# Attention scores as fp32 products of 32 rows in four banks, one projection per unit, and the weights W_ih loaded and split early

## The reference, cut to what matters

```python
xn = rms_norm(x, g_norm) * (1 + scale) + shift         # x [16, 256, 512], scale and shift from cond @ W_emb
q, k, v = split(xn @ W_qkv)                             # 16 heads, d = 32
logits = rms_norm(q, g_q) @ rms_norm(k, g_k).T * d ** -0.5
o = softmax(logits) @ v
x1 = x + o + o @ W_out
gi = x1 @ W_ih + b_ih                                   # GRU, 256 steps one after the other
r, z = sigmoid(gi_r + h_r), sigmoid(gi_z + h_z)         # h_* from h @ W_hh + b_hh
n = tanh(gi_n + r * h_n)
h = (1 - z) * n + z * h
out = x1 + h
```

## Time and profile before

| what | value |
|---|---|
| median of 3 runs | 1945.35 us (1941.71 to 1947.37) |
| the profiled execution, its own time | 1951.58 us |
| its span, first to last instruction | 1949.8 us |
| PE busy | 1796.5 us, 92% |
| DVE busy | 1285.5 us, 66% |
| ACT busy | 855.8 us, 44% |
| POOL busy | 391.2 us, 20% |
| mean granted TensorE clock | 0.969 of full |

### The profile page before, as it was taken

One profiled execution on the slowest core, in us unless ns is written; L12 is line 12 of the kernel. 1 busy time (PEld: TensorE's weight loads), 2 busy tenths in 40 slices (PEclk: granted clock), 3 DMA queues, 4 the chain that ended last, 5 costly groups with the idle time before them and its releaser, 6 DMA issues.

```text
span 1949.8 us, 59362 instructions
## 1 busy us (share of the span) xinstructions
PE 1796.5 (92%) x23337; PEld 1279.7 (66%) x23337; DVE 1285.5 (66%) x5150; ACT 855.8 (44%) x3116; POOL 391.2 (20%) x473
## 2 busy tenths in 40 slices
PE   5699999999999999588999999999999999999996
PEld 4577777777777777455666666666666666666663
DVE  4687777777777777544666666666666666666665
ACT  2466665566665655522333333333333333333333
POOL 3333333333333332110111111111111111111111
PEclk8799999999999999788999999999999999999999
DMA  5555554545544454623434343434343343434341
GB/s 192 129 134 127 124 125 121 127 120 126 122 123 119 121 128 115 174 50 77 76 75 67 74 77 67 81 69 78 67 76 65 76 73 67 83 67 78 62 69 16
DMA packets 155069, 185.94 MB, mean 95 GB/s; under 512 B 18124, under 2 KB 116632, under 8 KB 154792
## 3 DMA queue, kind: packets, MB, share of 16 engines
q1 hardware_dynamic: 154792, 182.14, 43.0%
HBM read 73.01 MB, written 41.94 MB: 59 GB/s over the span
## 4 chain that ended last, share of the span: by engine, by line
PE 86%; issue 4%; DVE 3%; DMA 3%; SPq 2%; POOL 1%; ACT 1%; POOLq 0%; DVEq 0%
PE ps L673 37%; PE ps L654 16%; PE ps L424 13%; PE ps L460 5%; PE ps L496 4%; PE ps L480 3%; PE ps L449 3%; PE ps L486 2%; PE ps L432 1%; SPq L260 1%; DVE xf L702 1%; DMA wst<-in_L_cond_W_ih_dram 1%; DMA GI<-gscr 1%; PE ps L506 1%; PE ps L412 1%
## 5 line engine op out<-in xcount | busy, mean ns | idle before, releaser
L673 PE MATMUL ps<-whh,hT 128*32 128x192 f32 x16384 | 753.4, 329 | 26.4 <-DVE hT L965 13.9
L673 PEld LDWEIGHTS ps<-whh,hT 128*32 128x32 f32 x16384 | 486.7, 110 | 297.7 <-issue 80.2
L1247 POOL TENSOR_TENSOR outG<-hG,GI 128x128 f32<-128x128 f32 x256 | 116.5, 455 | 1038.1 <-DVE hG L958 1038.1
L1138 ACT ACTIVATE v<-ps 128x128 f32<-128x128 f32 x512 | 139.5, 272 | 413.7 <-PE ps L673 413.7
L937 DVE SCALAR_TENSOR_TENSOR v<-v,ps 128x64 f32<-128x64 f32 x512 | 111.0, 217 | 285.0 <-ACT v L1138 285.0
L1142 ACT ACTIVATE v<-v 128x64 f32<-128x64 f32 x512 | 131.2, 256 | 304.5 <-DVE v L945 304.5
L742 DVE TENSOR_REDUCE nmx<-ps 128x2 f32<-128x512 f32 x256 | 175.2, 685 | 116.8 <-PE ps L449 115.7
L1041 ACT ACTIVATE P<-ps,nmx 128x256 f32<-128x256 f32 x512 | 240.9, 483 | 8.6 <-DVE nmx L742 8.6
L1190 POOL TENSOR_TENSOR rq<-msq,mh 128x16 f32<-128x16 f32 x64 | 187.2, 2925 | 5.4 <-POOL msq L1186 0.2
L954 DVE TENSOR_TENSOR v<-v,v 128x64 f32<-128x64 f32 x512 | 115.1, 225 | 105.7 <-ACT v L1142 105.7
L449 PE MATMUL ps<-kst,qst 128*128 128x256 f32 x512 | 130.7, 339 | 47.5 <-issue 47.5
(11 more groups left out here) (107 smaller groups left out, 2506.0 us busy)
## 6 DMA issues: line engine op xcount, KB each, us to landing
gscr<-nat SPq DMA_DIRECT2D x96, 256.0 KB, 2.7
GI<-gscr SPq DMA_DIRECT2D x128, 192.0 KB, 6.6
kst<-kh SPq DMA_DIRECT2D x128, 128.0 KB, 2.4
kst<-kl SPq DMA_DIRECT2D x128, 128.0 KB, 2.4
qst<-qh SPq DMA_DIRECT2D x128, 128.0 KB, 2.5
qst<-ql SPq DMA_DIRECT2D x128, 128.0 KB, 2.4
xb<-in_x_dram SPq DMA_DIRECT2D x16, 512.0 KB, 4.9
xres<-in_x_dram SPq DMA_DIRECT2D x32, 256.0 KB, 3.2
```

The costliest lines, as they stand in the source:

```text
L673: last = pe.matmul(ps[32 * j:32 * j + 32, q, 0:192], hT[:, 32 * c:32 * c + 32], whg[:, c, :, 128 * j + 64 * q:128 * j + 64 * q + 64], star ...
L1138: s.activation(v_rz[:, q, :], ps[:, q, 64:192], ACT.Tanh, scale=0.5).then_inc(s_tr, 1)
```

## The change

- Scores: no parts and no stacks. The turned q and k are kept as fp32, `qT` and `kT`, for two batches. `scores(U)` makes four products of 32 rows, one for each head of the unit, from partitions 32j to 32j+31, each into its own bank (0 to 3), after both exponential pairs of the unit before.
- The banks: `PASS` uses banks 7 and 6; `pO` and `pR` move into bank 5, single, beside the second half of the turned probabilities, so `turn_p` waits for `scale` of the unit before.
- The order: PE makes scores(U+1), `turn_p(U)`, the fillers (at most one projection or output projection in a unit), `times_v(U)`. DVE takes `scale(U-1)` first, then both maxima, its copy, the reciprocals, and only then what belongs to the fillers. The turned q and k are copied by ACT (`keep_turned`) in place of DVE. `raw` and its square are two steps on ACT.
- `xh` and `xl` are double. The squares of x have a tile of their own, `xsq`.
- W_ih is loaded when batch 1 begins and one of its 12 blocks is split in each of the batches 2 to 13.
- After the last unit the input products for the first 16 steps are made (72 matmuls) before the GRU starts; the other 1080 pieces are laid 4 or 5 to a step.

```diff
-        PASS += [("turn", _n, 0, 1), ("project", _n, 0, 0), ("turn", _n, 1, 1), ("project", _n, 1, 0), ("turn", _n, 0, 0),
-                 ("project", _n, 0, 2), ("turn", _n, 1, 0), ("project", _n, 1, 2)]
+        PASS += [("turn", _n, 0, 1), ("project", _n, 0, 0), ("turn", _n, 1, 1), ("project", _n, 1, 0), ("project", _n, 0, 2)]
     if _m < NB:
-        PASS += [("rows", _m, 0), ("rows", _m, 1)]
+        PASS += [("rows", _m, 0)]
+    if _n < NB:
+        PASS += [("turn", _n, 0, 0), ("project", _n, 1, 2)]
+    if _m < NB:
+        PASS += [("rows", _m, 1)]
     PASS += [("out", _b, 0)]
-BANK = {p: (7, 3)[k % 2] for k, p in enumerate(PASS)}
+BANK = {p: (7, 6)[k % 2] for k, p in enumerate(PASS)}
...
+            def scores(U):
                 b, c, i = U // 8, U % 4, U % 8 // 4
...
+                if U:
+                    pe.wait_ge(s_ex, 2 * U)
+                for j in range(4):
+                    q = slice(32 * j, 32 * j + 32)
+                    last = pe.matmul(pS[j], qT[b % 2][q, i, c, :], kT[b % 2][q, :, c, :], start=True, stop=True)
                 last.then_inc(s_S, 1)
...
+            scores(0)
             for U in range(NU):
                 b, u = U // 8, U % 8
                 n, m = b + 1, b + 2
                 if U + 1 < NU:
-                    scores(U + 1, 0)
-
+                    scores(U + 1)
+                turn_p(U)
+                if u == 0 and b:
+                    passed(("turn", b, 1, 0))
+                elif u == 2 and b:
+                    passed(("out", b - 1, 1))
+                elif u == 5 and n == NB or u == 7 and n < NB:
+                    passed(("out", b, 0))
                 if n < NB:
                     if u == 0:
                         passed(("project", n, 0, 1))
-                    elif u == 2:
+                    elif u == 1:
+                        passed(("project", n, 1, 1))
+                    elif u == 3:
                         passed(("turn", n, 0, 1))
                         passed(("project", n, 0, 0))
-                    elif u == 3:
+                    elif u == 4:
+                        passed(("turn", n, 1, 1))
                         passed(("project", n, 1, 0))
-                    elif u == 4:
+                    elif u == 5:
                         passed(("project", n, 0, 2))
-                    elif u == 5:
+                        if m < NB:
+                            passed(("rows", m, 0))
+                    elif u == 6:
+                        passed(("turn", n, 0, 0))
                         passed(("project", n, 1, 2))
...
+                        if m < NB:
+                            passed(("rows", m, 1))
+                times_v(U)
...
+            for tt in range(2):
+                for g in range(3):
+                    for k in range(GP):
+                        gate_piece(tt, g, k)
+                turn_x1(tt + 1, F[2])
...
+                if U:
+                    scale(U - 1)
                 if U + 1 < NU:
                     maxima(U + 1, 0)
                     maxima(U + 1, 1)
...
                 if U:
                     low(U - 1)
...
+                if b and u == 0:
+                    out_sum(b - 1, 0)
+                elif b and u == 3:
+                    out_sum(b - 1, 1)
+                if n < NB:
+                    if u == 1:
+                        squares(n, 0, 1)
+                    elif u == 2:
+                        squares(n, 1, 1)
+                        normalize(n, 0, 1)
+                    elif u == 3:
+                        normalize(n, 1, 1)
+                    elif u == 4:
+                        squares(n, 0, 0)
+                        if m < NB:
+                            x_scale(m)
+                    elif u == 5:
+                        squares(n, 1, 0)
+                        normalize(n, 0, 0)
+                    elif u == 6:
+                        if m < NB:
+                            affine(m, 0, BANK["rows", m, 0])
+                        normalize(n, 1, 0)
+                    elif u == 7:
+                        if m < NB:
+                            affine(m, 1, BANK["rows", m, 1])
+                        if 2 <= b < 2 + 3 * KC:
+                            wih_low((b - 2) // KC, (b - 2) % KC)
```

More of the change, by code:

```diff
@@ L32 @@
     _n, _m = _b + 1, _b + 2
+    if _b:
+        PASS += [("turn", _b, 1, 0)]
     if _n < NB:
@@ L143, in cond_resid_kernel @@
         E = sb("E", [128, NB])
[L144 removed]
+        assert base[0] <= a_qk
         base[0] = a_P
@@ L320, in _ @@
             load_x(1)
-            stack(0, 1)
-            stack(0, 0)
             for b in range(NB):
[L325 to L329, removed]
+                if b + 2 < NB:
+                    load_x(b + 2)
+                if b == 1:
+                    sp.wait_ge(s_wsd, 3)
+                    sp.wait_ge(s_ss, 1)
                     for g in range(3):
@@ L367, in _ @@
                         sp.dma_start(whh[32 * j:32 * j + 32, :, D:3 * D], w[:, :, 0:2 * D]).then_inc(s_lwh, 16)
+                if b:
+                    store_x1(b - 1, 0)
+                    load_residual(b - 1, 1)
+                    store_x1(b - 1, 1)
+                load_residual(b, 0)
+            store_x1(NB - 1, 0)
+            load_residual(NB - 1, 1)
+            load_x1(0)
+            load_x1(1)
+            load_gx(0)
+            load_x1(2)
+            store_x1(NB - 1, 1)
+            for g in range(3):
+                store_gate(0, g)
+            load_g(0)
+            load_x1(3)
+            for g in range(3):
+                store_gate(1, g)
+            load_g(1)
+            load_x1(4)
             o_v = out.rearrange("b (t s) (j f) -> t j b s f", s=ST, j=4)
@@ L555, in passed @@
                     out_proj(*a)
-            def first_gate(g):
-                bank = (7, 3, 7)[g]
-                if g == 0:
-                    emptied(pe, ("out", NB - 1, 0))
-                    pe.wait_ge(s_1c, 2)
-                    pe.wait_ge(s_wsl, 3 * KC)
-                elif g == 2:
-                    pe.wait_ge(s_gb, 1)
-                for c in range(KC):
-                    for m, (xp, wp) in enumerate(((x1h, wih_h), (x1l, wih_h), (x1h, wih_l))):
-                        last = pe.matmul(ps[:, bank, :], xp[:, 0, c, :], wp[:, c, g * D:(g + 1) * D],
-                                         start=(c == 0 and m == 0), stop=(c == KC - 1 and m == 2))
-                last.then_inc(s_g, 1)
-            scores(0, 0)
-            scores(0, 1)
+            scores(0)
             for U in range(NU):
@@ L617, in _ @@
-                turn_p(U)
-                if u == 5 and m < NB:
-                    passed(("rows", m, 0))
-                if n == NB:
-                    if u == 4:
-                        passed(("out", b, 0))
-                    elif u == 5:
-                        emptied(pe, ("out", b - 1, 1))
-                        turn_x1(0, ps[:, 3, :])
-                    elif u == 6:
-                        first_gate(1)
-            times_v(NU - 1)
+                        if m < NB:
+                            passed(("rows", m, 1))
@@ L657, in gate_piece @@
                     last.then_inc(s_g, 1)
+            emptied(pe, ("out", NB - 1, 0))
+            emptied(pe, ("out", NB - 2, 1))
+            turn_x1(0, F[2])
+            passed(("out", NB - 1, 1))
+            for tt in range(2):
+                for g in range(3):
+                    for k in range(GP):
+                        gate_piece(tt, g, k)
+                turn_x1(tt + 1, F[2])
             first_seed()
@@ L928, in _ @@
             low(NU - 1)
+            x1_low(0, F[2])
+            out_sum(NB - 1, 1)
+            for tt in range(2):
+                for g in range(3):
+                    keep_gate(tt, g, F[(3 * tt + g) % 2])
+                x1_low(tt + 1, F[2])
             for t in range(T):
@@ L1022, in keep_raw, with keep_turned @@
                 s.activation(sq[:, i, :], raw[:, i, :], ACT.Square).then_inc(s_sq, 1)
+            def keep_turned(b, i, g):
+                bank = BANK["turn", b, i, g]
+                r = ps[:, bank, :].rearrange("p (c t) -> p c t", c=KC)
+                s.wait_ge(s_qT, nth(b, i, g) + 1)
+                if b >= 2 and i == 0:
+                    s.wait_ge(s_S, 8 * (b - 1))
+                if g == 0:
+                    s.activation(qT[b % 2][:, i, :, :], r, ACT.Copy, scale=gqs).then_inc(s_ev[bank], 1)
+                else:
+                    s.copy(kT[b % 2][:, i, :, :], r).then_inc(s_ev[bank], 1)
             def keep_v(b, i):
@@ L1091, in _ @@
                 n, m = b + 1, b + 2
-                k = 3 * u - 5
-                if n == NB and 0 <= k < 3 * KC:
-                    wih_high(k // KC, k % KC)
+                s.wait_ge(s_P, 2 * U + 1)
+                s.copy(PT[:, 0:2, :, :], pP[:, 0:2, :, :]).then_inc(s_pa, 1)
+                if U + 1 < NU:
+                    exps(U + 1, 0)
+                    exps(U + 1, 1)
```

(2 more changed lines are left out.)

442 lines of the change are left out of this document (129 added, 313 removed).

## The result

The changed kernel takes 1967.76 us (median of 4 runs, 1966.32 to 1969.27) where the kernel before takes 1946.36 (4 runs, 1941.71 to 1947.62): a ratio of 1.0114, 95% interval 1.0095 to 1.0133. It is slower, and the whole interval lies above 1. The profiled execution took 1966.32 us, its span 1964.5 against 1949.8 before, so the two spans differ by 14.7 us; the medians differ by 21.4, because the profiled execution of the kernel before (1951.58 us) was 5 us over its median and this one 1 us under its own.

A forecast was written before the change was run, and what follows sets the result against it. PE's own work plus its standing still bounds the batches, a step loop the GRU. Start -5, batches 1 to 13 +45, batch 14 +5, last batch -7 and GRU -18.5 make +19.5: 1965 us, range 1922 to 2050.

The forecast's parts named there:

- Batches 1 to 13: The 13 middle batches: 51.1 us each against 47.65, +45 us in all, bounds +11 and +85.
- The stops: PE waits before projections for DVE to empty banks: 1.8 us at u = 0 and 3, 2.1 at u = 6.
- PE's own work: PE's fp32 scores take 0.57 us a unit against 0.48, bounds 0 and +0.09; taken as +0.4 us a batch.
- The clock: PE's stops cause none to three clock drops a batch at 1.67 us each; 1.3 taken, 2.2 us.
- The start and batch 0: DVE's first maxima no longer wait 4.4 us for scores held up by stacks: -5 us.
- Batch 14: No `rows` there, so two stops: 47.0 us against 42.3, +5.
- The last batch and the first gates: From the last batch into the GRU: 59 us against 66.8, -7, between -12 and -2.
- The GRU: First 18 steps no longer wait for the gates of steps 9 to 16; a step stays 4.16 us: -18.5 us.
- The stacks' DMAs: The 32 stack transfers go, and with them PE's stop ahead of each batch's first scores.
- (b): Rival: PE's weight loads of 128 columns don't run abreast, +0.53 us a unit, 2031 us; 12%.
- (c): Rival: PE's row tiles don't run abreast at all, +1.4 us a unit, 2140 us; 11%.
- (a): Rival: PE's stops don't pull the clock down and scores cost what they did, 48.5 us a batch, 1929 us; 22%.

The follow-up runs named there:

- Experiments 1 to 3: Changed kernel, out_sum at the head of DVE's unit (1925.77 us); affine of u = 6 too (1886.16); then the last batch's u = 3 sum back behind low (1880.87).
- experiment 4: Changed kernel with every unit's scores issued twice into the same banks, as extra work: 2021.94 us, ratio 1.038.
- experiment 2: Changed kernel with out_sum (u = 0 and 3) and affine (u = 6) at the head of DVE's unit: 1886.16 us, ratio 0.969.
- experiment 1: Changed kernel with out_sum at the head of DVE's unit at u = 0 and u = 3: 1925.77 us, ratio 0.9886.
- Experiment 6: Changed kernel with the gates of steps 9 to 16 made in the GRU's first steps again, as before: 1986.8 us, ratio 1.0193.

## Why the prediction was right, and where it was right by luck

The forecast was 1965 us, the result 1967.76; on the spans +19.5 against +14.7. Batches 1 to 13 came out 4.8 us above their forecast of +45, the other stages together 10 below theirs. Step by step:

**The stops, +5.8 us a batch: right in cause and near in size.** They stand where the prediction put them, released by `out_sum` at u = 0 and u = 3 and by `affine` at u = 6, 1.69, 1.69 and 2.00 us where it said 1.8, 1.8 and 2.1. DVE's chain after the scores was forecast as 0.60 for each long operation and 0.60 for the short ones, and the trace has 1.29 + 0.60 + 0.54 + 0.61. To the 5.4 of standing still comes 0.27 behind each stop, where the overlap of the first product is missing; 6.2 in all. Experiments 1 to 3 show the cause: an edit of DVE's order alone takes away all but the 0.47 us at u = 0.

**PE's own work, +0.4 us a batch: mis-sized.** Two rounds of 0.23 for the eight records were right (0.44, experiment 4). The change of tiling was wrong: 0.1 was taken once, ahead of the scores, and turn_p was left at its 0.87. It is about 0.2 ahead and 0.15 behind. The unit's scores take 0.64 instead of twice 0.24, turn_p 1.02 instead of 0.87: 0.31 x 8 = 2.5 a batch. The batches of experiment 2 say nearly the same: 45.13 less the 0.47 at u = 0 is 44.7, 1.9 over the 42.73 of before, and those 42.73 hold the same surcharge twice already (0.27 and 0.23, behind the two waits of that batch, 1.10 and 1.77 us), so 2.4. The row that could have said so was in the trace of before: the one transpose of rB behind times_v took 0.26, where the eight of turn_p took 0.87, 0.11 each. In the chain of waits:

```profile
425.87 0.26 PE ps L486
```

**The clock, +2.2 us a batch: mis-sized, the other way.** Five falls at 1.6 in 13 batches are 0.6 us a batch, not 1.3 falls in each. The prediction took the length of a stop for what decides, with the line between 1.77 and 2.11 us. In the changed kernel the stops of 2.00 us pulled the clock down 4 times in 14, the 27 of 1.69 us never, and the one of 1.95 us (u = 3 of batch 11) did; in experiment 1 those of 2.00 us 4 times in 14 again; at 2.30 it was 4 of 14 in one place and 14 of 14 in the other. The trace of before already had the row that crosses the line. In batch 6, where PE waits for the next batch's first scores, it reads

```profile
394.28 0.47 PE L449 MATMUL ps<-kst,qst 128*128 128x256 f32 x2 [1.76 <-issue]
```

and this stop did pull the clock down (a mean of 0.51 of full from 394.7 to 398.1 us), where 1.77 us in batch 1 had left it whole. So length sets a chance, not a line.

The last two errors cancel, and that is luck: 0.4 + 5.8 + 2.2 = 8.4 forecast, 1.9 + 6.2 + 0.6 = 8.7 measured, each over 42.7; the measured 669.3 / 13 = 51.5 is 8.8 over it. With only the clock put right the forecast would have been 21 us lower (13 x 1.6), 1944 us; with only PE's work put right, 20 us higher (13 x 1.5), 1985 us.

**The start and batch 0, -5: measured -8.5.** The maxima start at 61.28 right behind the bias, and not 4.4 us after it, and the first PT copy of all comes 12 us earlier; batch 0 itself then takes 46.5 us, with PE busy for 42.79 of them, where it took 43.2 before (78.2 to 121.5): it has a stop at u = 6 too, which the forecast of this stage left out.

**Batch 14, +5: measured +5.4. The last batch and the first gates, -7: measured -8.4.** Most of the units that ACT bounds take 3.8 us, between the 3.6 and the 4.0 that the prediction weighed; 58.4 us came out where it said 59.

**The GRU, -18.5: measured -23.6.** The step without pieces is still 4.15 us, and there is no stop at step 8. Experiment 6 prices the early gates by themselves at 19.0 us in all and at 20.9 in this stretch. Of the other 2.7 us, 1.9 are an output projection of the last batch, whose products stood between the GRU's first two steps before (the transposes of h for the next steps started 4.79 us apart there, 855.86 and 860.65, and 2.87 after).

**The stacks' DMAs.** The stop for them has gone: from 185.94 to 118.75 MB moved, and no wait ahead of a batch's scores. The gain is seen once the new stops are gone: a batch of 45.13 instead of 47.65, and 1880.87 us in all. Not all of it is the stacks'. The kernel before also waited for `affine`, 1.1 us in a batch, and the order of experiment 2 has no such wait; the prediction does not name it.

```profile
PE ps L496 <- DVE xf L702: 15.3, 14, 1.1
```

The change as made lost 5.4 + 0.8 us a batch to the order of a list on DVE.

Of the rivals, (b) and (c) fall by experiment 4, and (a) held for the clock nearly as far as it went (0.6 us a batch, under the 0.8 at which it said that the sum is zero), but not in its other half, scores at no cost.

## What to carry to other kernels

When buffers are dealt out in turn, a new order of pieces changes who must empty what before whom: go through the list of each emptying engine and put what a tight bank waits for at its head, behind a product that ended in the unit before. Check the ends of the loop apart from its middle: moving the sum of u = 3 won 1.95 us a batch and lost 3.9 in the last one, where the load it needs was late. And count each change between tiled and whole-array products as a cost of its own, in both directions; one return to the whole array less in each unit won 14 us here, and no work was left out for it.

## What the runs showed that I had not expected

- A single 128x128 fp32 transpose takes 0.26 us behind column tiles and 0.11 behind the whole array; eight behind row tiles take 1.02 where they took 0.87. Both are 0.15 us; only the first was shown by moving it.
- Four row tiles of 32 rows and 256 fp32 columns, in four banks, run abreast at 0.22 us a round.
- Behind a stop of 1.7 to 2.0 us twelve fp32r products take 3.03 us instead of 2.75, with the granted clock at 2.4 GHz throughout, and behind a wait of 0.2 us they take 3.00: the surcharge comes with any wait and hardly depends on its length.
- Stops of the same 2.30 us pulled the clock down to 1.2 GHz in 4 of 14 cases at one place of the batch and in all 14 at another; with 1.3 us of other work added in unit 6, in none and in all 14.
